# Two changes in one program: gate rows in two halves in front of attention, and paths, normalisation and logits by pairs of groups inside the first expert units

## The reference

```python
x = x + tanh(g_xattn[0]) * mlstm(layernorm(x), ctx, ctx, ifgate_w, ifgate_b, outnorm_w)
x = x + tanh(g_ffn[0]) * quantized_ffn(layernorm(x), W1, b1, W2, b2)
x = x + tanh(g_xattn[1]) * dtw_expand(ctx, layernorm(x))   # small[i] added along the best path
x = x + tanh(g_ffn[1]) * experts(layernorm(x), gate_w, w1, b1, w2, b2)

# mlstm: pre = 15 * tanh((concat(q, k, v) @ ifgate_w.T + ifgate_b) / 15)
#   lf = cumsum(log_sigmoid(f_pre)); log_d[t, s] = lf[t] - lf[s] + i_pre[s], s <= t
#   m = max_s log_d; scores = (q @ k.T) / sqrt(DH) * exp(log_d - m)
#   out = scores @ v / max(|sum(scores)|, exp(-m)), normalised per head
# experts (8 experts, 512 hidden): logits = x @ gate_w.T
#   kth = the 3072nd smallest logit of all; gates = logits * (logits >= kth)
#   out = sum_e gates_e * (gelu(x @ w1_e.T + b1_e) @ w2_e.T + b2_e)
```

## Time and profile before

| | us |
|---|---|
| median of 3 runs (lowest to highest) | 738.99 (738.05 to 739.28) |
| profiled execution | 738.34 |
| its span | 736.5 |
| PE busy | 574.9 (78% of the span) |
| DVE busy | 568.8 (77%) |
| ACT busy | 406.3 (55%) |
| POOL busy | 128.4 (17%) |
| mean granted PE clock | 0.879 |

### The profile page before, as it was taken

How to read it: one execution, slowest core, us unless ns; L and a number is a source line. 1 busy time by engine, 2 the same in 40 slices (tenths; PEclk the granted TensorE clock), 3 DMA queues, 4 the chain that set the end, 5 groups by cost and what they waited for, 6 DMA issues and landing times.

```text
span 736.5 us, 17181 instructions
## 1 busy us (share of the span) xinstructions
PE 574.9 (78%) x6419; PEld 402.7 (55%) x6419; DVE 568.8 (77%) x1737; ACT 406.3 (55%) x764; POOL 128.4 (17%) x163
## 2 busy tenths in 40 slices
PE   3758998726455810093689999999999999999997
PEld 2433443312144710092586777776777777777776
DVE  7866788989969479997965665677876888887675
ACT  2766786688772532284345656655545454545452
POOL 4000442504000000000047777700000000000000
PEclk9969999857758975586758999999999999999999
DMA  8100000000010000050000000000000000010000
GB/s 226 45 0 2 2 4 1 2 0 0 1 57 1 3 1 0 1 171 2 0 1 1 2 2 1 2 2 1 16 1 17 1 0 15 0 43 0 16 1 16
DMA packets 19675, 12.13 MB, mean 16 GB/s; under 512 B 1148, under 2 KB 18456, under 8 KB 19608
## 3 DMA queue, kind: packets, MB, share of 16 engines
q1 hardware_dynamic: 19608, 11.25, 5.5%
HBM read 9.15 MB, written 2.10 MB: 15 GB/s over the span
## 4 chain that ended last, share of the span: by engine, by line
PE 64%; DVE 25%; ACT 7%; issue 2%; SPq 1%; DMA 1%; DVEq 0%
PE PS L1669 8%; PE PS L1668 8%; PE PS L1667 8%; PE PS L1651 8%; PE PS L1652 8%; PE PS L1653 7%; DVE A L1178 3%; DVE Bm L1149 3%; PE PS L1462 3%; PE PS L1472 2%; ACT A L595 2%; DVE Bm L738 2%; PE PS L1481 1%; PE PS L1580 1%; DVE A L1143 1%
## 5 line engine op out<-in xcount | busy, mean ns | idle before, releaser
L701 ACT ACTIVATE A<-PS,small_t 128x512 f32<-128x512 f32 x256 | 168.4, 688 | 118.9 <-PE PS L1653 117.3
L1669 PE MATMUL PS<-kT_w,A 128*128 128x128 bf16 x1024 | 174.8, 219 | 0.0
L1668 PE MATMUL PS<-kT_w,A 128*128 128x128 bf16 x1024 | 174.8, 219 | 0.0
L1667 PE MATMUL PS<-kT_w,A 128*128 128x128 bf16 x1024 | 174.8, 219 | 0.0
L1280 DVE TENSOR_TENSOR A<-A 128x512 bf16<-128x512 f32 x192 | 123.6, 689 | 7.8 <-ACT A L701 6.6
L1668 PEld LDWEIGHTS PS<-kT_w,A 128*128 128x128 bf16 x1024 | 100.2, 98 | 7.4
L1667 PEld LDWEIGHTS PS<-kT_w,A 128*128 128x128 bf16 x1024 | 100.2, 98 | 7.4
L1669 PEld LDWEIGHTS PS<-kT_w,A 128*128 128x128 bf16 x1024 | 100.2, 98 | 0.0
L1652 PE MATMUL PS<-A,xn_w 128*128 128x512 bf16 (+1 forms) x256 | 97.8, 382 | 0.0
L1653 PE MATMUL PS<-A,xn_w 128*128 128x512 bf16 (+1 forms) x256 | 97.7, 382 | 0.0
L1651 PE MATMUL PS<-A,xn_w 128*128 128x512 bf16 (+1 forms) x256 | 97.7, 382 | 0.0
(11 more groups left out here) (335 smaller groups left out, 1142.6 us busy)
## 6 DMA issues: line engine op xcount, KB each, us to landing
slab<-in_L_ffn_w_dram SPq DMA_DIRECT2D x16, 256.0 KB, 3.1
xs<-in_x_dram SPq DMA_DIRECT2D x4, 512.0 KB, 5.7
cs<-in_ctx_dram SPq DMA_DIRECT2D x4, 512.0 KB, 6.5
out_dram<-xs SPq DMA_DIRECT2D x8, 256.0 KB, 2.5
Bm<-in_L_ffn_W_dram SPq DMA_DIRECT2D x2, 256.0 KB, 2.8
b2blk<-in_L_ffn_b_dram SPq DMA_DIRECT2D x12, 4.0 KB
onw_b<-n_L_xattn_outnorm_w_dram SPq DMA_DIRECT2D x1, 64.0 KB
ab_b<-in_L_ffn_b_dram SPq DMA_DIRECT2D x1, 64.0 KB
```

The costliest lines, as they stand in the source:

```text
L701: act.activation(hf[:, e % 2, c, :], bank(c), ACT.Gelu_apprx_tanh, bias=b1).then_inc(S["h_gelu"], 1)
L1667: pe.matmul(o, hh[:, e % 2, c, t], w2h[:, e, c, :], start=(c == 0 and k == 0), stop=False, skip_group_check=True)
L1668: pe.matmul(o, hh[:, e % 2, c, t], w2l[:, e, c, :], start=False, stop=False, skip_group_check=True)
L1669: ins = pe.matmul(o, hl[:, e % 2, c, t], w2h[:, e, c, :], start=False, stop=(c == NC - 1), skip_group_check=True)
```

## The change

*Gates.* The rows of groups 0 to 3 and 4 to 7 are now separate tiles (`rows_of(j)`; the second lies in `Bm`) with their own copies, scans, cuts, remainders and masks, 512 columns at a time. The first half and the subtraction for the tokens are done before attention; the second half's cuts stand on ACT behind `weights_exp` of steps 1, 3 and 5, its remainders and masks on DVE in steps 2, 4 and 6, and PE waits for them ahead of step 16. The scaling of `expnm` moves into step 1. PE's `keep_warm` issues 8 products instead of 16. The copy that gave `tg_in_ready` goes.

*Paths and experts.* Distances, paths, expansions, additions, statistics, normalisation, turns and logits go by pairs of groups. Only groups 0 and 1 (and the expansions of 2 and 3) stand before the first unit; the rest stands between the parts of units (0, 0) to (0, 3). Mean and scale of a pair are computed without ACT: for the first on DVE (`first_scales`, a start value from the bits of the number and three Newton steps), for the others on POOL (`x4_scales`, with a power of -0.5 and one step). Even groups are normalised by DVE, odd ones by ACT. The expansions and logits use other banks, `x4f` has room for all groups, and the gelu table is loaded ahead of the distances.

*Search.* It begins in place 36 (a unit has eight places, the four parts of `hidden` and of `outputs`) and has a round every 16/3 places, `COUNT_AT`. The candidates' common part (`base`) is formed ahead of the wait for the counts.

```diff
+SEARCH_AT = 36
+COUNT_AT = {SEARCH_AT + (16 * n + 2) // 3: n for n in range(ROUNDS)}
...
 # POOL
+            def x4_scales(p):
+                w = slice(8 * p, 8 * p + 8)
+                t = lambda k: lnt[:, k, w]
+                pool.wait_ge(S["x4_stats"], p + 1)
+                pool.tensor_tensor(t(0), bns[:, w, 1], bns[:, w, 4], ALU.add)
...
+                link(pool.tensor_tensor(t(7), t(4), pm[:, 13:14].to_broadcast([P, 8]), ALU.pow))
...
+                pool.tensor_tensor(t(1), t(3), t(7), ALU.mult).then_inc(S["x4_scales"], 1)
+
+            split_x4(0)
+            for e in range(E):
+                if e <= 2:
+                    x4_scales(e + 1)
+                for c in range(NC):
+                    low(0, e, c)
+                if e >= 3:
+                    split_x4(e - 2)
+            split_x4(G4 - 2)
+            split_x4(G4 - 1)
...
 # ACT, attention steps
+                if b in (1, 3):
+                    cut(b // 2, 0, 1)
+                    cut(b // 2, 1, 1)
+                if b == 5:
+                    last_part(1)
...
 # ACT, experts
+            act.preload_act_table_set("gelu_apprx_tanh_and_others")
...
+            for g in range(7):
+                far(g)
+            x4_odd(1)
+            x4_keep(0)
+            x4_keep(1)
+            far(7)
             gelu(0, 0)
+            x4_odd(3)
+            for e in range(1, E):
+                gelu(0, e)
+                if e <= 3:
+                    x4_keep(2 * e)
+                    x4_keep(2 * e + 1)
+                keep_y(0, e - 1)
+                if e <= 2:
+                    x4_odd(2 * e + 3)
...
 # DVE, gates
+            keep_rows(0)
+            running_max(0)
+            dve.wait_ge(S["csq_done"], 2)
+            keep_rows(1)
+            left_over(0, 0, 0)
+            left_over(1, 0, 0)
+            running_max(1)
+            left_over(0, 1, 0)
+            left_over(1, 1, 0)
+            mask_rows(0)
+            max_tokens(0)
+            max_tokens(1).then_inc(S["m_tok_ready"], 1)
...
 # DVE, attention steps
+                if b in (2, 4):
+                    left_over(0, b // 2 - 1, 1)
+                    left_over(1, b // 2 - 1, 1)
+                if b == 6:
+                    mask_rows(1)
...
 # DVE, experts
+            path_of(0)
+            path_of(1)
+            add_expanded(0)
+            stats(0)
+            add_expanded(1)
+            link(stats(1))
+            first_scales()
+            dve.wait_ge(S["x4_scales"], 1)
+            dve.sem_inc(S["x4_stats"], 1)
+            x4_even(0)
+            for g in range(2, 6):
                 path_of(g)
...
+            for p in range(1, G4 // 2):
+                add_expanded(2 * p)
+                add_expanded(2 * p + 1)
+                stats(2 * p)
+                stats(2 * p + 1).then_inc(S["x4_stats"], 1)
+                keep_logits(2 * p - 2)
+                keep_logits(2 * p - 1)
+                if p == 1:
+                    path_of(6)
+                    path_of(7)
+                dve.wait_ge(S["x4_scales"], p + 1)
+                x4_even(2 * p)
...
             def round_end(n):
...
+                if n < ROUNDS - 1:
+                    link(next_base(n + 1))
+                dve.wait_ge(S["count_all"], n + 1)
                 link(dve.tensor_scalar(sel[:, 8:8 + w], bank(7, 0, w), KTH - 1.0, None, ALU.is_le, ALU.add, accum_out=sel[:, 4:5]))
                 link(ts(step, sel[:, 4:5], float(1 << SHIFT[n]), None, ALU.mult))
+                if n < ROUNDS - 1:
+                    v = digits(n + 1)
+                    dve.tensor_tensor(cand[:, 0:v], base[:, 0:v], step.to_broadcast([P, v]), ALU.bitwise_xor)
                 link(dve.tensor_tensor(key, key, step, ALU.bitwise_xor))
...
 # PE
-            keep_warm(7, 16)
+            keep_warm(7, 8)
...
+            def turn_x4(g):
+                pe.wait_ge(S["x4_odd" if g % 2 else "x4_even"], g // 2 + 1)
+                pe.wait_ge(S["expanded_added"], min(g + 3, G4) if g >= 2 else g + 1)
...
+            expand(0)
+            expand(1)
+            turn_x4(0)
+            turn_x4(1)
+            expand(2)
+            expand(3)
...
             hidden(0, 0)
+            expand(4)
+            expand(5)
+            hidden(0, 1)
+            turn_x4(2)
+            turn_x4(3)
+            outputs(0, 0)
+            expand(6)
+            expand(7)
+            hidden(0, 2)
+            turn_x4(4)
+            turn_x4(5)
+            outputs(0, 1)
+            hidden(0, 3)
+            turn_x4(6)
+            turn_x4(7)
+            outputs(0, 2)
```

More of the change, by code:

```diff
@@ L678, in _, with far @@
                     rest(n - 1)
+            act.preload_act_table_set("gelu_apprx_tanh_and_others")
             act.wait_ge(S["e_kept"], 1)
-            for g in range(G4):
+            def far(g):
                 for b in range(4 * g, 4 * g + 4):
@@ L1647, in hidden, with logits @@
+            def logits(g):
+                pe.wait_ge(S["x4_kept"], g + 1)
+                for k in range(4):
+                    b = 4 * g + k
+                    ins = pe.matmul(bank(6 + g % 2, E * k, E * k + E), x4f[:, g, P * k:P * k + P], small_t[:, 84:92], start=True, stop=True)
+                ins.then_inc(S["logits_done"], 1)
+            expand(0)
[4 more added lines that the diff above has]
+            expand(3)
             def hidden(blk, e):
```

300 lines of the change are left out of this document (174 added, 126 removed).

## The result

The changed kernel takes 733.0 us (median of 5 runs, 730.96 to 733.33) against 738.99 (5 runs, 736.9 to 741.37) for the one before: ratio 0.9904, 95% interval 0.9876 to 0.9933. The forecast was 731.0, range 725.0 to 736.5. The profiled execution took 732.16, its span 730.1.

The account below looks back on a forecast made before the run. PE was taken as the bound, busy without a gap from the first expert unit at 388 us. Terms -1.9 - 25.2 + 14.8 - 1.0 + 3.5 + 2 = -7.8 from 738.99 gave 731.2, stated as 731.0, range 725.0 to 736.5.

Parts of the forecast that it names:

- Part 1: Gates in halves before attention: first exponential 2.5 us earlier, 0.6 lost again; net -1.9 us (-2.5 to -0.5).
- Given back: Second half's cuts, remainders and mask rows within the first seven attention steps: 0 to 1.8 us lost, 0.6 taken.
- Start of the units: Before the first unit: with only two groups needed, its first hidden product starts at 363.0 instead of 388.2, -25.2 us.
- Extra PE work: Inside the units: the moved expansions, turns and logits cost PE 4.2 + 3.5 + 7.1 = +14.8 us.
- Waits: In the first units: PE waits because DVE and POOL hold each other up, +3.5 us (0.5 to 6).
- My walk: Stepping through the engines' queues in the first units: PE waits 2.6, 1.0 and 1.8 us at turns, 5.4 in all.
- Clock: At the units' start: PE's stretch at half clock gets shorter, -1.0 us (-2 to +1).
- Rival 3: Moved work between the units' products keeps PE's clock at 0.50: up to 33 us lost, 764; chance 0.05.
- Search: Search rounds, now closer together in the units: 0.1 to 0.2 us of waiting per round, +2 us (0 to +7).
- rival 2: The search becomes the bound: each of 17 rounds costs 0.5 us over budget, 8.5 us, so 737.7; chance 0.06.
- third copy: Sign in the units: the copy that keeps the third unit's output comes at about 401 us, 409.84 before.
- Attention steps of 2.35: Sign in the attention loop: steps still take 2.35 us each despite the added gate work.

Follow-up runs that it names:

- Experiment 6: Changed kernel with the second half's gate work spread over attention steps 2 to 6: 731.07 us, ratio 0.9883 to the kernel before.
- experiment 5: Changed kernel with the second half's mask rows in attention step 8 instead of 6 and ACT's last part in 6 instead of 5: 731.66 us.
- experiment 1: Two kernels: the kernel before with the new gate part alone, 737.86 us (ratio 0.9976); the changed kernel with the old gate part, 735.09 us (0.9919).
- experiment 2: Changed kernel with POOL waiting for DVE's even normalisation before its low halves in the first three units: 730.21 us, ratio 0.9861.
- Experiment 3: Changed kernel with POOL raising to the power twice in each pair's scales: 738.34 us, ratio 0.9981.
- Experiment 4: Changed kernel with the search's candidates formed by the old linked chain again: 733.6 us, ratio 0.9912.
- 7: Changed kernel with POOL's wait for the even normalisation, gate work spread over steps 2 to 6, and warming products in lots of 4 and 5: 729.34 us.
- 9: Changed kernel with POOL's wait, spread gate work, split warming products, DVE's own scales for all pairs and DVE's order mended: 728.35 us, ratio 0.9826.
- the second of 8: Changed kernel with POOL's wait, spread gate work, split warming products and DVE's own scales for all pairs: 730.35 us, ratio 0.9867.
- the first of 8: Changed kernel with POOL's wait for the even normalisation and DVE's own scales for all pairs: 728.8 us, ratio 0.9846.
- the gates alone: Kernel before with only the new gate part and 8 warming products: 737.86 us against 740.05, ratio 0.9976.

## Why the prediction was right, and where it was not

It was right in its sign, and 2 us from the measured median. Its main term and its account of the moved work hold. Three smaller terms don't: what the gates give back and the waits were under-sized, the search over-sized; and the first unit started 1.4 us earlier than forecast. That these partly made up for each other is luck.

1. *Part 1, -1.9: its loss was under-sized; the sum stays open between 0 and -2.* The gain was as worked out (2.0 to 2.8 in the profiles for 2.5; 2.0 where the clock stayed low, which I had named). The step that failed is "Given back", of which it says "I take 0.6 of their 0 to 1.8". I had spread the second half's work evenly against the mean free time of a step. It measured 2.0, over my upper end (18.4 in all six profiles with this gate part, 16.42 in both with the old one), all from the work in steps 5 and 6, where four masks, a remainder's mask and a reduction fall on DVE together and ACT has two tables more. Experiment 6 gets 1.7 of it back by moving the same operations one or two steps forward; experiment 5 shows that behind step 7 POOL spoils them. By the two profiles nothing is left of the gain; by the times of experiment 1 it is 1.1 to 1.8 us. The two aren't reconciled.
2. *Start of the units, -25.2: right, a little low.* 361.55 for 363.0, -26.6. The expansions 2 and 3 brought the clock up themselves (2.89 for sixteen products, where I had 3.6).
3. *Extra PE work, +14.8: right, a little high.* Logits come every 0.81 (taken 0.88), expansions 1.0, turns 0.6: 6.5 + 4.1 + 3.6 = 14.2.
4. *Waits, +3.5: under-sized.* They measured 3.46 + 2.75 = 6.2. My walk had given 2.6, 1.0 and 1.8, 5.4 in all, and I took less than it said. The mechanism was right: four DVE scalings beside four POOL operations take 4.04, one per operation, and experiment 2 removes the waits by keeping the two apart. The walk had the places only in part: no wait came at pair 4, and that at pair 2 ends with the addition behind the normalisation. The sentence of the Trainium skill in "SBUF — State Buffer", "Who interferes with whom", on the shared port pair stood beside this term: with POOL first, its upper end, which is what came (6.2 for 6). The power measured 1.68, above the 1.3 that I had as its bound from the trace; the scales still took 4.8, within 3.9 to 4.9, since the other steps were shorter. Experiment 3 shows what this chain is worth.
5. *Clock, -1.0: right in sign, some -0.3 by these two pieces.* The first unit gained the 2 us it used to lose; after the wait of 3.46 the clock fell to 0.50 and that cost about 1.7 (an estimate from 0.84 over the 11 us from 370 to 381). Another 0.6 left this stretch with the four counts, which the prediction didn't count here. Rival 3 (0.05) was right as a mechanism, not in size: it took the wait, not the turns. The turns in the units did not stay slow: eight of their products took 1.09 at a granted clock of 1.00 (396.76), where the first two turns, ahead of the units, took 1.97 for eight at 0.50 (357.17). What "TensorE: Matmul & The Clock Gate" of the Trainium skill says in "Part 4: PE-mode transpose", that the full clock does not engage for transposes, this trace does not bear out in this setting, between other products: the clock, once up, stayed up through them. Whether turns alone would bring it up, no run here shows; from 366 to 388 of the kernel before, turns and logits did not (0.50).
6. *Search, +2: wrong, measured 0 of waiting.* The budget was right (3.4 to 4.1, measured 3.46 and 4.15). The step that failed is the "0.1 to 0.2 of waiting per round": I had a round at 2.6 to 4.3 us, and it took 2.1 to 3.2 (3.8 once, at a long gap). The second exclusive-or took 0.15 right behind the first in every round, what I had put as "against" rival 2. Experiment 4 puts the old chain back, and then PE waits 0.8 us. Third copy to the end is 1.1 longer; the four counts that moved there make up some 0.6 of it (a unit took 5.41 us with a count and 5.27 without in the kernel before), the rest is not traced.

In all: distances to third copy predicted -25.2 + 14.8 - 1.0 + 3.5 = -7.9, measured -7.7; the front -1.9, measured +0.2 in these profiles; the rest +2, measured +1.1. Of what I had asked for as signs these came: the first exponential (57.19), the first product (0.45 earlier than the earliest I gave), DVE rows of 1 us, third copy (402.3 for 401). Attention steps of 2.35 did not (2.63 at the mean over steps 2 to 9), nor did the search's small waits.

## What to carry to other kernels

Moving preparatory work behind the point where the bound engine starts pays what it kept that engine waiting for, less its own length there; then each queue has to be walked, since the new neighbours decide: the same four DVE operations cost 1.11 or 4.04 us by whether POOL works beside them, and one semaphore that keeps the two apart was worth 3 us in the trace. Don't set moved work against the mean free time of a loop's step: read the steps that it lands in, one by one. And a wait of the matrix engine can have a second price, in clock, that is larger than the wait (some 4.9 us for 1.8 more of waiting in experiment 3).

## What the runs showed of the hardware that was not expected

- POOL's power of -0.5 on 128 x 8 elements takes 1.64 to 1.77 us where a product of that size takes 0.20.
- The clock's answer to a wait is not in proportion: 3.46 us idle, then 4 us at 0.57; 5.25 us idle, then 12 us at 0.50 with PE busy throughout; 2.53 us idle in the same run, then 8 us at 0.78 to 0.80, where 2.75 in the changed kernel cost nothing. It fell at 394 to 398 in four kernels (experiments 2, 7, 9 and the second of 8) in which PE had waited less than 1 us shortly before, and neither in the first of 8, with such a wait, nor in the changed kernel after its 2.75. What decides it stays open; no run was made on it alone.
- The eight warming products ended at 0.56 in the changed kernel's profile and at 0.89 (51 to 58 us) in that of the gates alone, with the same instructions; the first exponential came 0.75 earlier in the second, and so it did in the first kernel of experiment 8, whose front is the changed kernel's (12.69 after the copies).
- Of two small DVE operations back to back beside POOL, the first took 0.99 and the second 0.15 (0.15 in all 16 rounds); linked, the two took 0.70 and 0.97 in the round shown.
